# Weights loaded during layer 0's last tiles, gates kept in buffers of their own, five PSUM banks in the tail, and wider or split instructions in the rounds

## The chip, the cores and the metric

The kernel runs on one core of one Trainium2 chip. Its time is the device time of one launch in microseconds (us), taken as the median of the runs of one kernel.

A core has five engines with a program of its own each: TensorE (PE, whose weight loads are listed as PEld), VectorE (DVE), ScalarE (ACT), GpSimd (POOL) and SyncE (SP), which here only issues DMA transfers. [...]

## The reference, cut to what matters

Two layers over 16 sequences of 256 tokens with 128 features:

```python
xn = _layernorm(x)
s = _L0_attn_ref(xn, ...)               # LSTM-like scan: c = f*c + i*z, h = o*tanh(norm(c))
g = _silu(_L0_ffn_ref(xn, ...))         # tree FFN: 4 trees of depth 5, argmax over 4 children picks the row
x = x + s * g
xn = _layernorm(x)
s = _L1_attn_ref(xn, ...)               # gated delta rule, 16 heads of 8: S = S*exp(g) + k (v - kS) beta; o = qS
                                        # q, k, v = silu(conv4(xn @ W)); o * silu(xn @ Wg)
g = _silu(_L1_ffn_ref(xn, ...))         # 2 layers: local attention (8 heads of 64, window 64) and a GEGLU FFN
x = x + s * g

# inside the local attention
q = l2norm(q) * qs;  k = l2norm(k) * ksc
q = q*cos*scale + rotate_half(q)*sin*scale;  k = k*cos/scale + rotate_half(k)*sin/scale
attn = softmax(masked(8 * q @ k.T));  out = attn @ v
```

Everything is fp32.

## The kernel before, in words

**Layer 0** (`layer0_phase`, up to about 602 us, its tail to about 626). The 4096 tokens are 32 tiles of 128, in 8 groups of 4. The groups run through a software pipeline; `g` is the pipeline's step. The last two levels of the trees are not multiplied out: POOL gathers the chosen rows of a table by indirect DMA (L334, 256 of them, into `rows[4]` and `rows[5]`), DVE takes the dot products (`dots`, L753), ACT scales the rows by the activations (`gelu`, L634 and L639), and PE adds them up (`spread_rows`, L473) into `acc`. When the last group is through, its tail is a chain: ACT `tanh_f` (L676), DVE `raise_f` (L817, L818), PE `turn_f` (L480), DVE `merge` and the layer norm's statistics (`norms`, L826 to L855), ACT `put_rows` (L646, the normalised rows), PE `turn_m` (L396), ACT `keep_m` (L594), and then the projection `z` of the two gate weights on PE (L490), copied out by ACT (`keep_z`, L598) and stored by SP (L311). z(0) to z(6) belong to groups that are long done; z(7) is the last group's. They go into two PSUM banks in turn, `log_ps[h % 2]`, so that z(h) waits until keep_z(h - 2) is through. On ACT, keep_z(0) to keep_z(6) stand ahead of the last put_rows.

**Prepare** (`prepare_phase`, about 628 to 742 us). The convolution of four taps is done by PE with weights that carry the taps: DVE multiplies W and the taps into `wq`, `wk`, `wv` (L1180), and PE waits for it (`made`) before its 8 times 24 matmuls (L1025). ACT applies silu (L1052), SP stores the results to HBM scratch and loads them back in another layout (L965, L975). DVE, ACT and POOL then build the delta rule's operands, which SP stores (L982, L984). SP also issues 11 weight loads for the rounds (`m["late"]`, L994), one per step from the fourth on. At the end PE computes the output gates (L1034), ACT their silu (L1091) into buffers that alternate with the projections' staging buffers, and SP stores them (L1007). The last instruction of SP is a wait until the last gate has landed (L1015). A phase ends for all engines when all have ended (L76).

**The rounds** (`local_phase`, about 752 to 1554 us). 32 rounds, one for each of the local FFN's 2 layers and each of 16 sequences of 256 tokens, in a three-deep pipeline written out by hand: round t computes q, k, v for step t, attention for t - 1 and output projection and FFN for t - 2. POOL carries the delta rule beside it. In each round, every part is done twice (i or j = 0, 1, half of the tokens). ACT squares q and k (`squares`, L1724 and L1725); DVE rotates them (`cross` L2042 and L2043, `along` L2048, `add_parts` L2056). DVE takes the maxima of the scores (L2064), ACT the exponentials (`exps`, L1743, eight instructions over two banks), DVE the reciprocal of the sums (`inverse`, L2072) and the product (`normalise`, L2082, one instruction over both banks, after all eight). PE turns the probabilities (`turn_prob`, L1530), ACT copies them (`keep_pT`, L1751), PE multiplies by V (`weigh`, L1548), ACT copies the result (`keep_o`, L1757) out of the bank `o_ps`. That bank is then used by PE for `turn_qk` (L1482), the transposes of q, which ACT copies out (`keep_q`, L1784). `query` on DVE (L1988) is the delta rule's read-out, two instructions of 512.

## Time and profile before

| | us |
|---|---|
| median of 3 runs | 1553.08 (1552.3 to 1557.53) |
| the profiled execution | 1555.76 |
| its span, first to last instruction | 1554.0 |
| PE, DVE, ACT, POOL busy | 1306.3, 1296.0, 1235.3, 938.0 |
| layer 0 with its tail | to about 626 |
| prepare | 628.3 to 742 |
| rounds | 752 to 1554, of 23.54 each |

The page of a profile gives the busy time of each engine and, in 40 slices of the span, the busy share and the clock granted to PE. The views behind it are: windows (busy time of each engine in a stretch), the timeline (instructions in order of time, with the idle time of the engine before each and what ended it), the waits (who waited for whom), and the DMA issues (size, time to landing). L12 is line 12 of the kernel.

### The profile page before, as it was taken

The page shows a single profiled execution, that of the slowest core. Times are in us where ns is not written, and L with a number is a line of the kernel's source. Part 1 is how long each engine was busy: PE and PEld are TensorE (multiplying, and loading weights), DVE is VectorE, ACT ScalarE, POOL GpSimd, SP SyncE. Part 2 cuts the span into 40 slices and gives each one's busy share as a digit, 9 for nine tenths or more (in the row PEclk, how much of TensorE's full clock was granted, in tenths as well). Part 3 has the DMA queues.
Part 4 walks back from the last instruction along what each step waited for, and adds up shares of the span by engine and source line. Part 5 has one row for each costly group of instructions (what it writes and reads, how often), then busy time and mean ns, then how long its engine had stood idle before and what let it go on. Part 6 is the DMA issues. An engine that isn't in the chain of part 4 may idle for free.

```text
span 1554.0 us, 31376 instructions
## 1 busy us (share of the span) xinstructions
PE 1306.3 (84%) x9368; PEld 886.8 (57%) x9368; DVE 1296.0 (83%) x4362; ACT 1235.3 (79%) x3431; POOL 938.0 (60%) x1472
## 2 busy tenths in 40 slices
PE   5888878888797666897489999999999999999986
PEld 3555646566565443343256666666666666666665
DVE  3278897979888895488299999999999999999985
ACT  2367877979787886587289989989989989999985
POOL 0237464464645651078488778778778778777752
PEclk9999999999988856898699999999999999999998
DMA  3359677686868773499301101111101111111233
GB/s 111 107 183 335 222 280 248 218 297 213 314 204 285 286 274 109 136 286 315 122 22 34 44 11 44 43 44 34 43 13 44 44 44 34 19 36 44 67 94 111
DMA packets 156505, 210.33 MB, mean 135 GB/s; under 512 B 68272, under 2 KB 109616, under 8 KB 156208
## 3 DMA queue, kind: packets, MB, share of 16 engines
q0 software_dynamic: 36864, 134.76, 24.9%
q1 hardware_dynamic: 119040, 71.98, 16.8%
q8 instruction: 76, 1.25, 0.3%
q10 hardware_dynamic: 432, 1.59, 0.3%
q14 instruction: 93, 0.76, 0.2%
HBM read 168.97 MB, written 26.74 MB: 126 GB/s over the span
## 4 chain that ended last, share of the span: by engine, by line
PE 26%; ACT 14%; issue 6%; DVE 4%; POOL 2%; ACTq 0%; DVEq 0%; POOLq 0%
ACT lo_s_ps L1743 6%; PE lo_h_ps L1558 4%; PE lo_qk_ps L1454 4%; PE lo_s_ps L1510 3%; PE lo_o_ps L1548 2%; DVE prepared_then_rounds L2082 2%; ACT L1830 2%; ACT prepared_then_rounds L1801 2%; PE lo_ft_ps L1530 2%; PE lo_v_ps L1460 2%; PE lo_h_ps L1568 1%; PE lo_s_ps L1497 1%; PE lo_h_ps L1530 1%; ACT prepared_then_rounds L1751 1%; PE lo_o_ps L1530 1%
## 5 line engine op out<-in xcount | busy, mean ns | idle before, releaser
L334 POOL DMA_INDIRECT l_rows<-in_table,l_idx x256 | 256.5, 1002 | 293.9 <-DVE l_idx L795 131.4
L639 ACT ACTIVATE l_rows<-l_rows,l_act 128x128 f32<-128x128 f32 x1024 | 306.6, 390 | 2.1
L753 DVE CUSTOM_DVE_ANT_0 l_rows<-l_rows,xn_tok 128x128 f32<-128x128 f32 x1024 | 299.7, 362 | 6.5 <-DMA l_rows<-in_table,l_idx 4.9
L1743 ACT ACTIVATE lo_s_ps<-lo_s_ps,lo_nmx,lo_rn 128x128 f32<-128x128 f32 x504 | 219.7, 440 | 1.3 <-DVE lo_nmx L2066 0.9
L473 PE MATMUL l_acc<-ident,l_rows 128*128 128x128 f32 x1024 | 163.0, 307 | 55.6 <-ACT l_rows L639 34.3
L473 PEld LDWEIGHTS l_acc<-ident,l_rows 128*128 128x128 f32 x1024 | 129.4, 157 | 92.0 <-ACT l_rows L639 54.6
L439 PE MATMUL l_S<-pre,l_AT 128*128 128x144 f32 (+3 forms) x832 | 130.3, 308 | 25.9 <-ACT l_AT L630 24.7
L439 PEld LDWEIGHTS l_S<-pre,l_AT 128*128 128x128 f32 (+2 forms) x832 | 117.5, 208 | 56.4 <-ACT l_AT L630 40.0
L1454 PE MATMUL lo_qk_ps<-wqkv,lo_hT 128*128 128x512 f32 x256 | 126.6, 618 | 22.8 <-DVE lo_c L2056 11.5
L415 PE MATMUL l_log<-l_xT,top_in 128*128 128x512 f32 (+1 forms) x192 | 118.6, 711 | 19.1 <-issue 9.2
L1933 POOL TENSOR_TENSOR lo_de_kS<-lo_de_S,lo_de_ops 128x384 f32<-128x384 f32 x128 | 128.0, 1000 | 10.0
L1951 POOL TENSOR_TENSOR lo_c<-lo_c,lo_rn 128x512 f32<-128x512 f32 x64 | 66.8, 1044 | 97.1 <-ACT lo_rn L1792 94.5
L1743 ACT ACTIVATION_READ_ACCUMULATOR lo_s_ps<-lo_s_ps,lo_nmx,lo_rn 128x1 f32 x504 | 107.4, 213 | 0.0
L630 ACT ACTIVATE l_AT<-l_log,top_bias 128x512 f32<-128x512 f32 (+1 forms) x96 | 63.6, 679 | 55.0 <-PE l_log L431 48.1
L1939 POOL TENSOR_TENSOR lo_de_outer<-lo_de_dv,lo_de_ops 128x256 f32<-128x256 f32 x128 | 80.3, 628 | 10.0
L1454 PEld LDWEIGHTS lo_qk_ps<-wqkv,lo_hT 128*128 128x128 f32 x256 | 49.5, 195 | 60.4 <-issue 39.1
L2048 DVE TENSOR_TENSOR lo_qk_ps<-lo_qk_ps,tab 128x512 f32<-128x512 f32 x128 | 82.4, 690 | 0.0
L753 DVE DVE_READ_ACCUMULATOR2_ANT l_pick<- 128x1 f32 x1024 | 82.2, 80 | 0.0
L2056 DVE TENSOR_TENSOR lo_c<-lo_qk_ps,lo_c 128x512 f32<-128x512 f32 x128 | 81.7, 678 | 0.0
L2064 DVE TENSOR_REDUCE lo_nmx<-lo_s_ps 128x4 f32<-128x512 f32 x126 | 80.6, 681 | 0.0
L2021 DVE TENSOR_REDUCE lo_ss<-lo_sq 128x16 f32<-128x1024 f32 x64 | 77.3, 1207 | 3.4 <-ACT lo_sq L1725 3.4
L2082 DVE TENSOR_TENSOR prepared_then_rounds<-lo_s_ps,lo_rsum 128x1024 f32<-128x1024 f32 x63 | 77.1, 1224 | 2.3
(321 smaller groups left out, 3376.8 us busy)
## 6 DMA issues: line engine op xcount, KB each, us to landing
lo_VE<-lo_V SPq DMA_DIRECT2D x64, 128.0 KB, 2.8
scratch_ops<-prepared_then_rounds SPq DMA_DIRECT2D x4, 1792.0 KB, 7.5
lo_de_ops<-scratch_ops SPq DMA_DIRECT2D x16, 448.0 KB, 4.2
l_rows<-in_table,l_idx POOLq DMA_INDIRECT x256
scratch_qo<-prepared_then_rounds SPq DMA_DIRECT2D x8, 512.0 KB, 8.7
lo_de_qo<-scratch_qo SPq DMA_DIRECT2D x16, 256.0 KB, 4.6
x_tok<-in_x SPq DMA_DIRECT2D x8, 256.0 KB, 5.2
scratch_x<-x_tok SPq DMA_DIRECT2D x8, 256.0 KB
```

The costliest lines, as they stand in the source:

```text
L334: pool.indirect_dma_start(rows[L][:, r % SLOTS, p, :], None, a[f"table{L}"], bass.IndirectOffsetOnAxis(ap=at[:, p:p + 1], axis=0)).then_in ...
L415: ins = pe.matmul(log_ps[n % 2][0:width_of(k), :], w["top_in"][:, at_of(k):at_of(k) + width_of(k)], xT[:, h % 3, :], start=True, stop=(d = ...
L439: mm = lambda out, q, j, c0, c1, start: pe.matmul(out, at(q, j), w["top_out"][0:width_of(q), q, c0:c1], start=start, stop=True, skip_group ...
L473: ins = pe.matmul(out, rows[L][:, r % SLOTS, p, (FAN + f) * D:(FAN + f + 1) * D], m["ident"][:], start=False, stop=(L == 5 and k == PICK - ...
L639: ins = act.activation(z, z, ACT.Copy, scale=actv[L][:, r % 2, k:k + 1])
L753: ins = dve.tensor_tensor_reduce(z, z, x, 1.0, bias, ALU.mult, ALU.add, accum_out=pick[L][:, r % 2, k:k + 1])
L1454: ins = pe.matmul(dst, hT[:, u % 2, at], m["wqkv"][:, u // B, k * INNER:(k + 1) * INNER], start=True, stop=True)
L1743: ins = act.activation(here, here, ACT.Exp, scale=rn[:, v % 2, j, 2 * k + e:2 * k + e + 1], bias=nmx[:, j, e, k:k + 1], accum_out=sums[:, ...
L1933: link(pool.tensor_tensor(kS[:], both, by_key(n, U0, 3), ALU.mult))
L2048: dve.tensor_tensor(heads(src[:]), heads(src[:]), rot(u, i, a, 0, 0, DH), ALU.mult).then_inc(rotated.sem, 1)
L2056: dve.tensor_tensor(c1[:, i, w], src[:], c2[:, w], ALU.add).then_inc(done.sem, 1)
L2082: dve.tensor_tensor(prob[:, j].rearrange("p e k t -> p (e k) t"), z, rsum[:, j, :].unsqueeze(2).broadcast_to([P, 2 * NP, P]), ALU.mult).th ...
```

## The change

- At the start of ACT's program the table of the gelu functions is loaded (`preload_act_table_set`).
- In layer 0's tail z goes into five banks instead of two. z(0) to z(4) are issued by PE before the last two `spread_rows`; keep_z(0) and keep_z(1) stand between tanh_n and tanh_f, and keep_z(2) to keep_z(6) behind tanh_f as before.
- Eight of the eleven late weight loads (wqkv, wo, w1, w2, center, mean_mat, WgT, WoT: 1536 + 512 + 682 + 384 + 128 + 3 x 64 KB = 3434 KB) are issued by SP in layer 0, once spread_rows(4, 31) is done, into the memory of `rows[4]`. They stand ahead of keep_x(7). SP waits for them at the phase's end.
- The taps are multiplied into the weights by DVE in layer 0 (`weigh_taps`, three instructions), ahead of the last raise_f, in place; prepare loses these instructions, and PE the wait for them.
- In prepare, several temporaries and the gates' buffers lie in the memory of the rounds' `qT` and `kT`. ACT no longer waits for the projections' stores before a gate's silu, PE no longer waits for the late weights, and SP no longer waits for the gates' landing; that wait goes to ACT ahead of the rounds' first keep_q and to SP ahead of the load of the gates. The operands' layout in `qo` has packets of 1024 bytes where it had 512.
- In the rounds q and k are handled together: squares is one instruction of 1024 (2 of 512), cross 2 of 512 (4 of 256), along 1 of 1024 (2 of 512), add_parts 1 of 1024 (2 of 512), the maxima 1 of 1024 (2 of 512), query 1 of 1024 (2 of 512). inverse and normalise go the other way: one reciprocal of 4 and one product of 512 for each bank, each after its own four exponentials; turn_prob waits for its own bank's half.

The diff's core:

```diff
@@ layer0_phase
+        z_ps = [log_ps[0][:], log_ps[1][:], S[:, 0:2, :]..., S[:, 2:4, :]..., gate_ps[:]]
+        NZ = len(z_ps)
...
-            for h in range(3, NG):
+            for h in range(3, NG - 1):
                 keep_x(h)
+            sp.wait_ge(spread[4].sem, spread[4].after(NT - 1))
+            for k in WEIGHTS:
+                sp.dma_start(m[k], a[k]).then_inc(weights_in, 16)
+            keep_x(NG - 1)
...
+            sp.wait_ge(weights_in, 16 * len(WEIGHTS))
...
             for g in range(NG + 5):
+                for h in range(NZ) if g == NG + 3 else ():
+                    z(h)
...
-                for h in range(NG - 1) if g == NG + 4 else ():
+                for h in range(NZ, NG - 1) if g == NG + 4 else ():
                     z(h)
...
+            act.preload_act_table_set("gelu_and_others")
             act.wait_ge(halved.sem, 1)
...
                     tanh_n(g - 3)
+                for h in (0, 1) if g == NG + 2 else ():
+                    keep_z(h)
+                if on(g - 3):
                     tanh_f(g - 3)
-                for h in range(NG - 1) if g == NG + 2 else ():
+                for h in range(2, NG - 1) if g == NG + 2 else ():
                     keep_z(h)
...
+            def weigh_taps():
+                dve.wait_ge(pre_in, 16 * len([k for k in SHAPES1 if k not in PRE_EARLY]))
+                for x in "qkv":
+                    taps = m[f"conv_{x}"]
+                    dve.tensor_tensor(taps, m[f"W{x}T"].unsqueeze(1).broadcast_to([P, TAPS, P]), taps, ALU.mult)
@@ prepare_phase
-        gate_buf = [flat(stage[x][:, k]) for k in (0, 1) for x in "qkv"] + [flat(m[f"conv_{x}"]) for x in "qk"]
+        gate_buf = [m[x].rearrange("p a k t -> p (a k t)")[:, k * GW:(k + 1) * GW] for x in ("qT", "kT") for k in range(4)]
...
             sp.wait_ge(late.sem, 16 * len(m["late"]))
-            sp.wait_ge(gate_stored.sem, gate_stored.after(NG - 1))
...
-            pe.wait_ge(made.sem, 1)
...
-            pe.wait_ge(late.sem, 16 * len(m["late"]))
...
-                if g < 6:
-                    act.wait_ge(y_stored[x].sem, y_stored[x].after(n))
@@ local_phase
-                act.activation(sq[:, i, 0:INNER], q_ps, ACT.Square)
-                act.activation(sq[:, i, INNER:], k_ps, ACT.Square).then_inc(sq_ready.sem, 1)
+                act.activation(sq[:, i, :], flat(qk_ps[:]), ACT.Square).then_inc(sq_ready.sem, 1)
...
+                if (v, i) == (0, 0):
+                    act.wait_ge(m["gate_stored"].sem, m["gate_stored"].after(NG - 1))
...
-                for a, src in both:
-                    dve.wait_ge(crossed.sem, crossed.after(u, 2 * i + a + 1))
-                    dve.tensor_tensor(heads(src[:]), heads(src[:]), rot(u, i, a, 0, 0, DH), ALU.mult).then_inc(rotated.sem, 1)
+                dve.wait_ge(crossed.sem, crossed.after(u, i + 1))
+                dve.tensor_tensor(heads, heads, rot(u, i, 0, 0, DH), ALU.mult).then_inc(rotated.sem, 1)
...
+                for e in (0, 1):
+                    at, n = slice(e * NP, (e + 1) * NP), 2 * j + e + 1
...
+                    dve.wait_ge(prob_ready.sem, prob_ready.after(v, n))
+                    dve.reciprocal(rsum[:, j, at], sums[:, j, at]).then_inc(rsum_ready.sem, 1)
...
+                    dve.tensor_tensor(prob[:, j, e], z, rsum[:, j, at].unsqueeze(2).broadcast_to([P, NP, P]), ALU.mult).then_inc(pn_ready.sem, 1)
```

## Rows read from the trace of the kernel before

**Rows 1.** The page: the group of the exponentials (busy, mean ns of one).

```profile
L1743 ACT ACTIVATE lo_s_ps<-lo_s_ps,lo_nmx,lo_rn 128x128 f32<-128x128 f32 x504 | 219.7, 440 | 1.3 <-DVE lo_nmx L2066 0.9
```

**Rows 2.** Windows, one round: busy PE, PEld, DVE, ACT, POOL; PE clock, DMA share, GB/s.

```profile
1027.50:1051.04 23.54, 21.66 (x198) 15.13 (x197) 22.62 (x43) 21.35 (x62) 17.98 (x35) 1.00 0.28 70
```

**Rows 3.** Timeline, one round: start, duration, instruction, idle time before it and its releaser.

```profile
1054.39 0.20 DVE L2072 RECIPROCAL lo_rsum<-lo_sums 128x8 f32<-128x8 f32 x1 [0.39 <-ACT lo_s_ps L1743]
1054.63 0.64 ACT L1724 ACTIVATE lo_sq<-lo_qk_ps 128x512 f32<-128x512 f32 x1
1054.63 1.22 DVE L2082 TENSOR_TENSOR prepared_then_rounds<-lo_s_ps,lo_rsum 128x1024 f32<-128x1024 f32 x1
1055.60 0.64 ACT L1757 COPY prepared_then_rounds<-lo_o_ps 128x512 f32<-128x512 f32 x1
1055.79 0.42 DVE L2042 TENSOR_TENSOR lo_c<-lo_qk_ps,tab 128x256 f32<-128x256 f32 x1
1055.91 0.66 PE L1530 MATMUL lo_h_ps<-ident,prepared_then_rounds 128*128 128x128 f32 x4 [0.37 <-DVE prepared_then_rounds L2082]
1056.40 0.60 PE L1482 MATMUL lo_o_ps<-ident,lo_c 128*128 128x128 f32 x4
1057.04 0.59 ACT L1784 COPY lo_qT<-lo_o_ps 128x512 f32<-128x512 f32 x1 [0.32 <-PE lo_o_ps L1482]
1057.12 1.29 DVE L2048 TENSOR_TENSOR lo_qk_ps<-lo_qk_ps,tab 128x512 f32<-128x512 f32 x2
1062.04 2.32 DVE L1988 TENSOR_TENSOR lo_de_qS<-lo_de_S,lo_de_qo 128x512 f32<-128x512 f32 x2
```

**Rows 4.** Timeline, ScalarE at the start of the program.

```profile
9.96 1.28 ACT L646 ACT_TABLE_LOAD   x1 [9.96 <-DVE l_half L855]
```

**Rows 5.** Timeline, the end of layer 0.

```profile
607.95 0.69 DVE L817 SCALAR_TENSOR_TENSOR l_t<-l_t,l_acc 128x512 f32<-128x512 f32 x1 [7.94 <-ACT l_t L676]
610.46 8.55 PE L490 MATMUL l_log<-xT_pad,pre 128*32 128x512 f32 x14
615.85 0.16 DVE L855 SCALAR_TENSOR_TENSOR l_half<-l_mv,l_rstd 128x4 f32<-128x4 f32 x1
619.04 0.58 ACT L598 COPY xn_tok<-l_log 32x512 f32<-32x512 f32 x1 [0.34 <-PE l_log L490]
619.53 1.64 ACT L646 ACTIVATE xn_tok<-x_tok,l_half,l_rstd 128x128 f32<-128x128 f32 x4
```

**Rows 6.** Windows around the last gathers and in the steady part, columns as in rows 2.

```profile
585.00:594.00 9.00, 3.74 (x14) 2.54 (x15) 9.00 (x47) 7.20 (x23) 5.91 (x6) 0.65 0.81 291
594.00:600.00 6.00, 4.21 (x18) 3.01 (x17) 6.00 (x44) 4.30 (x15) 0.00 (x0) 0.50 0.00 1
525.00:545.00 20.00, 11.08 (x44) 7.42 (x44) 17.96 (x114) 14.05 (x44) 14.86 (x17) 0.67 0.99 368
```

**Rows 7.** Timeline, ScalarE's activations of the last two tiles' rows.

```profile
595.67 0.22 ACT L634 ACTIVATE l_act<-l_pick 128x16 f32<-128x16 f32 x1 [2.12 <-DVE l_pick L753]
601.08 0.21 ACT L634 ACTIVATE l_act<-l_pick 128x16 f32<-128x16 f32 x1
```

**Rows 8.** DMA issues: transfer, queue, count, size, us from issue to landing.

```profile
wqkv<-in_wqkv SPq DMA_DIRECT2D x1, 1536.0 KB, 7.6
```

**Rows 9.** Timeline, the start of the preparing phase.

```profile
628.34 0.69 DVE L1180 TENSOR_TENSOR pr_wq<-pre 128x512 f32<-128x512 f32 x1 [12.33 <-PEq L76]
630.29 6.26 PE L1025 MATMUL pr_ps<-xT_pad,pr_wq 128*128 128x512 f32 x8 [5.80 <-DVE pr_wv L1180]
```

**Rows 10.** SyncE's waits in 700:800: waited for, us in total, times, longest.

```profile
SPq L1015 <- DMA scratch_gate<-pre: 7.2, 1, 7.2
```

**Rows 11.** Timeline, SyncE's last issues of prepare.

```profile
740.43 2.53 SPq L1007 DMA_DIRECT2D scratch_gate<-pre  x2
```

**Rows 12.** Timeline, ScalarE: the rounds' start and their first copy of q.

```profile
751.98 1.28 ACT L1830 ACT_TABLE_LOAD   x1 [14.50 <-PEq L76]
...
769.04 0.59 ACT L1784 COPY lo_qT<-lo_ft_ps 128x512 f32<-128x512 f32 x1
```

More of the change, by code:

```diff
@@ L205, in layer0_phase @@
         idx = {4: sb("l0_idx4", [P, 2, GT * TREES], U32), 5: sb("l0_idx5", [P, SLOTS, TREES], U32)}
-        rows = {L: sb(f"l0_rows{L}", [P, SLOTS, TREES, ROW]) for L in (4, 5)}
+        rows = {4: m["wide"][:].rearrange("p (s t x) -> p s t x", s=SLOTS, t=TREES), 5: sb("l0_rows5", [P, SLOTS, TREES, ROW])}
         pick = {L: sb(f"l0_pick{L}", [P, 2, PICK]) for L in (4, 5)}
@@ L485, in z @@
                     pe.wait_ge(pre_early, 16 * len(PRE_EARLY))
-                pe.wait_ge(log_kept.sem, len(order))
+                    pe.wait_ge(log_kept.sem, len(order))
+                    pe.wait_ge(ftop_kept.sem, ftop_kept.after(NG - 1))
+                    pe.wait_ge(gate_kept.sem, gate_kept.after(NG - 1))
                 pe.wait_ge(m_kept.sem, m_kept.after(h))
-                if h >= 2:
-                    pe.wait_ge(z_kept.sem, z_kept.after(h - 2))
-                pe.matmul(log_ps[h % 2][0:2 * NH, :], m["Wab"], m["xT_pad"][:, h * SG:(h + 1) * SG, TAPS - 1:], start=True, stop=True).then_inc(z_full.sem, 1)
+                if h >= NZ:
+                    pe.wait_ge(z_kept.sem, z_kept.after(h - NZ))
+                pe.matmul(z_ps[h % NZ][0:2 * NH, :], m["Wab"], m["xT_pad"][:, h * SG:(h + 1) * SG, TAPS - 1:], start=True, stop=True).then_inc(z_full.sem, 1)
             pe.wait_ge(early, 16 * len(EARLY0))
@@ L884, in _ @@
                     dots(5, GT * (g - 3) + 0)
+                if g == NG + 3:
+                    weigh_taps()
                 if on(g - 4):
@@ L1177, in sums @@
                 dve.tensor_reduce(ss[:], sq[:], AX.X, ALU.add).then_inc(ss_ready.sem, 1)
-            for x in "qkv":
-                ins = dve.tensor_tensor(wj[x][:], m[f"W{x}T"].unsqueeze(1).broadcast_to([P, TAPS, P]), m[f"conv_{x}"], ALU.mult)
-            ins.then_inc(made.sem, 1)
             dve.wait_ge(neg_exp.sem, 1)
@@ L1415, in _ @@
             sp.wait_ge(ss_floored.sem, ss_floored.after(LAST))
+            sp.wait_ge(m["gate_stored"].sem, m["gate_stored"].after(NG - 1))
             for n in range(4):
@@ L1452, in project @@
                 at = slice(i * P, (i + 1) * P)
-                for k, dst in ((0, q_ps), (1, k_ps)):
-                    ins = pe.matmul(dst, hT[:, u % 2, at], m["wqkv"][:, u // B, k * INNER:(k + 1) * INNER], start=True, stop=True)
+                for k in (0, 1):
+                    ins = pe.matmul(qk_ps[:, k, :], hT[:, u % 2, at], m["wqkv"][:, u // B, k * INNER:(k + 1) * INNER], start=True, stop=True)
                 ins.then_inc(qk_full.sem, 1)
@@ L1465, in turn_qk @@
                 else:
-                    pe.wait_ge(q_summed.sem, q_summed.after(v, i + 1))
+                    pe.wait_ge(parts.sem, parts.after(v, i + 1))
                 dst = qk_bank(2 * i + w)
@@ L2227, in layer1 @@
         x_scope.close()
-        for k, s in SHAPES2.items():
-            if k not in ONCE2:
-                m2[k] = ctx.enter_context(nc.sbuf_tensor(k, s, F32, side="right" if k == "wqkv" else "left"))
-        m2["tab"] = ctx.enter_context(nc.sbuf_tensor("tab", [P, LAYERS, 2, 2, 2, DH], F32))
+        m2["tab"] = m["tab"].rearrange("p (l a c t j) -> p l a c t j", l=LAYERS, a=2, c=2, t=2)
         m2["b1"] = ctx.enter_context(nc.sbuf_tensor("b1_local", [P, 6 * LAYERS], F32))
@@ L2380, in program @@
             at += n
+        m["wide"] = res("wide", [P, SLOTS * TREES * ROW])
+        at = 0
+        for k, s in WIDE.items():
+            n = math.prod(s[1:])
+            m[k] = m["wide"][:, at:at + n]
+            if len(s) == 3:
+                m[k] = m[k].rearrange("p (a b) -> p a b", a=s[1])
+            elif len(s) == 4:
+                m[k] = m[k].rearrange("p (a b c) -> p a b c", a=s[1], b=s[2])
+            at += n
         gathers = keep.enter_context(Phase(nc))
+        m["gate_stored"] = Step(gathers, nc, "gate_stored", 16)
         m["x_stored"] = Step(gathers, nc, "x_stored", 16 * NG)
```

139 lines of the change are left out of this document (63 added, 76 removed).

## The prediction, made before the changed kernel ran

> **What bounds the kernel now.** The page comes first: PE and DVE are busy 84% and 83% of the span (the table above), so no engine bounds the whole, and the kernel is read by stage.
>
> The rounds are half of the span: 32 of 23.54 us. In one of them PE is busy 21.66, DVE 22.62 and ACT 21.35 us [rows 2]. None fills the period: a round is a cycle of waits across three engines, and DVE has only 0.92 us of idle time in it. The timeline shows where the waits stand [rows 3]. DVE waits 0.39 us for the last exponential, does the reciprocal and one wide normalise of 1.22, and PE waits 0.37 for that before it turns the probabilities (L1530). Next PE turns q (L1482 at 1056.40), and ACT waits 0.32 for that (L1784). But L1482 writes the bank that ACT's copy L1757 empties: the copy runs from 1055.60 for 0.64 and ends at 1056.24, 0.16 before L1482 starts.
>
> The joins are read in the timeline too. At the start ACT sits idle until 9.96 and then loads a table for 1.28 us ahead of its first rows [rows 4]. At layer 0's end the z's occupy PE for 8.55 us with 14 instructions; the norm's scaling is ready at 616.01 (615.85 + 0.16), but ACT starts put_rows only at 619.53, since the last of keep_z(0) to (6), at 619.04, stands ahead of it [rows 5]. Prepare starts at 628.34 with DVE's three products, and PE starts at 630.29 behind them [rows 9]. At its end SP waits 7.2 us for the gates' stores to land [rows 10], and nobody else works.
>
> **The change, part by part.** Minus is time saved.
>
> *Start.* The first table load moves under ACT's 9.96 us of idle time, and L646 starts 1.28 earlier [rows 4]. Layer 0 has one more load, which ran beside PE's work; it stays or goes and costs nothing either way. -1.3, bounds -1.3 and 0.
>
> *Layer 0's tail.* With five banks and z(0) to z(4) issued early, keep_z(2) to (6) run right behind tanh_f: five copies of 0.58 in the 8 us from tanh_f to 616. Put_rows starts when the scaling is ready, 616.01 and some 0.25 for the semaphore, instead of at 619.53: -3.3, with all behind it (turn_m, keep_m, z(7), its copy and store) in step [rows 5]. The two copies that now stand ahead of tanh_f take about 1.0 together, where tanh_f had waited 0.7 for PE: +0.2, bounds 0 and +0.5.
>
> The weights work against it. SP issues 3434 KB when spread_rows(4, 31) ends, at about 585, while tile 31's gathers are under way: from 585 to 594 the DMA engines move 291 GB/s, 2.6 MB, and then nothing, so the gathers land by about 593.5 [rows 6]. Their first readers are tile 31's dot products, which follow tile 30's; ACT takes up tile 30 at 595.67 and tile 31 at 601.08, the second without idle time before it [rows 7]. A tile's dots take some 4.4 us, so they may start at 596.7 and delay nobody: that is when the gathers are needed. If both streams get half of the engines until the gathers are through, these land after 5.2 MB. At the 368 GB/s of the steady part [rows 6] that is 14 us from 585, 599, a loss of 2.4; at 291 it is 603, a loss of 6; if the weights queue up behind, nothing. The weights have longer rows than the gathers' mix, so I lean to the quick side and take +2.0, bounds 0 and +6. They are all down by 610 at worst (a landing of 1536 KB took 7.6 us [rows 8]), well ahead of the phase's end. keep_x(7), which SP now issues behind eight more transfers, isn't due before 612.
>
> [...]
>
> weigh_taps is three instructions, the 1.95 us between 628.34 and 630.29 in prepare [rows 9]. In layer 0 DVE runs them between the last dots, at 600, and raise_f, before which it sits idle 7.94 us [rows 5]: 0, and 1.95 if that cover were gone. The whole tail: -3.3 + 0.2 + 2.0 = -1.1, bounds -3.3 and +3.
>
> *Prepare's start.* PE starts right with the phase instead of 1.95 later [rows 9], and follows on without a gap until its projections are through: -1.95. The last fifth of prepare belongs to DVE and POOL, fed through loads; with 3.4 MB less in the queues it may close up a bit more, or soak up a part. Bounds -1 and -3.
>
> *The gates' landing.* The phase ends with SP's last issue, 740.43 + 2.53 = 742.96 [rows 11], and the wait of 7.2 us goes [rows 10]. Next late are DVE and PE, which are through at 741.5. The wait comes back on ACT ahead of the rounds' first keep_q, but that copy starts 17 us after the rounds do, 769.04 against 751.98 [rows 12], and the gates land 7.2 us after SP's last issue: covered by 8 us. Behind it on ACT stand all copies of the first rounds, so without the cover it would cost the full wait. -7.2, bounds -8 and -6.5.
>
> *The rounds.* Four exponentials of 0.44 with their read-outs take 1.8 us [rows 1]: the first bank's are done 1.8 before the second's. DVE's earlier work ends at 1054.00 (0.39 before 1054.39), so the first half of normalise (0.20 and some 0.65) is ready at about 1054.95 instead of 1055.85, and PE's wait of 0.37 is gone [rows 3]. The second half is ready as before, over 2 us ahead of its reader. PE then comes to L1482 at about 1056.03, but the bank is free at 1056.24, or 0.05 earlier, as two squares of 0.64 (1054.63 to 1055.60, 0.97) become one of 1024, which I put at 0.92. So L1482 moves from 1056.40 to about 1056.24, and ACT's next copy with it: -0.16.
>
> Against that stands DVE's sum. A pair of 512 takes 1.29, one product of 1024 takes 1.22 [rows 3]: the split costs 0.07 and a second reciprocal of 0.20, twice a round, +0.55. The merging gives back 0.07 each for along, add_parts and the maxima (twice) and for query, and about 0.1 for cross, whose four of 256 take 1.33 (1055.79 to 1057.12), twice: -0.7. Net about -0.1, beside 0.92 of idle time. along now waits for both halves of cross: 0 to +0.1. 30 rounds of 0.16 are -4.8; bounds 0 and -9 (0.30 a round).
>
> *Ramp, last rounds, clock.* Normalise by bank helps where PE waits for it in the first and last rounds, 0.4 each, and PE's shorter pause between the phases may save 0.3 of slow clock: -1.1, bounds 0 and -2.
>
> Sum: -1.3 - 1.1 - 1.95 - 7.2 - 4.8 - 1.1 = -17.4. Against the profiled execution, 1555.76, that is 1538.3; it lay 2.7 above the median of the runs, and 1.8 of it lie outside its span. Against the median, 1553.08, it gives 1535.7, and I say **1536**.
>
> **The rivals.**
>
> 1. *The weights take the gathers' time.* Tile 31's rows land at 603, and the tail is +3 instead of -1.1: 1536 + 4.2 = 1540. For it: the gathers get no more than 291 GB/s when alone [rows 6]. Against: 368 at other times, and the order of issue, since most of the gathers are on their way before the weights. [...]
>
> 2. *The rounds gain PE's whole wait.* 30 times 0.37 = 11.1 in place of 4.8: 1529.5. It needs L1757 to move up with the rest. Against: ACT's instructions from 1054.63 on follow each other without idle time up to 1056.7 [rows 3], so only shorter work can move it.
>
> 3. *The rounds gain nothing.* The split uses up DVE's 0.92, or the merged instructions wait for the later of q and k: 1536 + 4.8 = 1541.
>
> 4. *Slower: DVE becomes the bound.* The wide instructions may take more than the sum of their parts. Query is the place to look: two of 512 took 2.32 together, beside POOL [rows 3], and it becomes one over broadcast operands. Outside the rounds 12.6 us are gained. The rounds must get longer by 0.4 us each, 12.6 / 32, to bring the time back to 1553, and by 0.54 to be slower by 0.3%. With 0.92 of idle time to fill first, DVE's work must grow by 1.3 to 1.5 us a round; about 16 us of it are touched, so by 8 or 9%. Then the time is 1558 and more.
>
> 5. *The join gives less.* SP's last issues took 1.27 each (2.53 for two [rows 11]); if the queues push back as hard without the weights' late loads, or more since the gates now come sooner, the end moves by 4 instead of 7.2: 1539.
>
> **How the numbers follow.** The forecast, 1533 to 1538.5: 0.48. Rival 1: 0.14. Rival 2: 0.10. Rival 3: 0.13. Rival 5: 0.07. Rival 4: 0.05. A smaller growth of DVE's work that eats most of the gain: 0.03. The range reaches toward rival 2's side and beyond rivals 1 and 3, to where one of them meets a weak join: 1528 to 1544. A measurement of this kernel can tell 0.3%, 4.7 us, from no change. Faster than 1548.4 are the forecast and rivals 1, 2, 3 and 5, 0.92, less 0.02 for two of them together: 0.90. Within: 0.05. Slower: 0.05.
>
> **What would show it.** In the profile of the changed kernel: no load between 9.96 and ACT's first rows; put_rows 0.25 behind the scaling; tile 31's dots with or without a wait for a DMA, the tail's whole question; PE's first L1025 right at the phase's start; no wait of SP for the gates, and 2 us from its last issue to the rounds; a period of 23.38 with L1530 not waiting for normalise and L1482 right behind the end of L1757. The prediction is wrong if the period is over 23.5 or under 23.2, if DVE has no idle time left in a round, or if ACT waits over 3 us for tile 31.

## The result, and where the time went

The changed kernel takes 1542.23 us (median of 4 runs, 1538.92 to 1543.03) where the kernel before takes 1553.03, 10.8 us less. The ratio on record is 0.9917, 95% interval 0.9888 to 0.9945; the two medians by themselves give 0.9930, inside it. On another chip, where the kernel before took 1521.53, the changed kernel took 1508.75, 12.8 less, and the ratio was 0.9924 (0.9901 to 0.9946). The gain is clear of the noise, and under 1%. The forecast was 1536, range 1528 to 1544. The direction and the range held; the gain is 0.6 of the forecast one.

The page of the changed kernel, busy time by engine:

```profile
span 1541.0 us, 31140 instructions
PE 1294.8 (84%) x9368; PEld 881.3 (57%) x9368; DVE 1270.8 (82%) x4138; ACT 1228.2 (80%) x3366; POOL 945.8 (61%) x1472
```

The time is read by stage, from marks in the timelines: the last two `tanh_f` of layer 0, the start of prepare, the end of SyncE's last issue in prepare, the rounds' first instruction, and the table load that opens each round. The first column needs a word: it is 571 and 581 us in two profiles of the kernel before, and 565 and 533 in two of the changed kernel, so layer 0's body wanders by more than this change is worth. The later stages agree far better. "28 rounds" is from the fourth round's table load to the last one's, "period" the mean of the ten rounds from the eleventh on, "end" from the last round's table load to the end of the span.

| profile | last but one tanh_f | to the last | to prepare | prepare | join | first 3 rounds | 28 rounds | period | end |
|---|---|---|---|---|---|---|---|---|---|
| before | 571.3 | 36.0 | 21.0 | 114.7 | 9.0 | 62.0 | 659.6 | 23.544 | 80.5 |
| before_again | 580.6 | 36.1 | 20.7 | 114.1 | 9.6 | 63.9 | 659.5 | 23.542 | 80.6 |
| before_preload | 576.4 | 36.1 | 21.2 | 114.8 | 9.1 | 61.9 | 659.3 | 23.533 | 80.6 |
| changed | 564.7 | 42.9 | 18.1 | 112.5 | 2.0 | 62.1 | 657.5 | 23.484 | 81.3 |
| changed_again | 533.5 | 42.9 | 18.1 | 112.6 | 2.0 | 61.8 | 657.1 | 23.467 | 79.5 |
| no_preload | 570.9 | 43.2 | 18.0 | 113.3 | 1.8 | 62.0 | 657.1 | 23.467 | 80.3 |
| split_only | 537.3 | 36.1 | 19.2 | 114.7 | 8.6 | 62.1 | 660.1 | 23.593 | 80.3 |
| merged_only | 576.8 | 41.3 | 18.1 | 113.3 | 1.8 | 62.4 | 659.7 | 23.569 | 80.4 |
| one_normalise | 587.1 | 42.6 | 18.1 | 112.8 | 1.8 | 62.6 | 661.6 | 23.629 | 81.1 |
| weights_after_gathers | 578.6 | 36.3 | 18.1 | 112.6 | 2.0 | 62.0 | 657.2 | 23.469 | 79.1 |
| weights_in_prepare | 576.1 | 36.3 | 18.1 | 111.9 | 2.0 | 61.9 | 654.0 | 23.357 | 81.2 |
| keep_o_first | 578.4 | 42.5 | 18.1 | 111.9 | 2.0 | 62.0 | 654.0 | 23.358 | 79.2 |
| both_moves | 534.8 | 36.7 | 18.1 | 113.0 | 1.8 | 61.9 | 654.0 | 23.355 | 80.0 |
| keep_k_first | 535.7 | 36.2 | 18.1 | 112.5 | 1.9 | 63.9 | 658.4 | 23.503 | 80.2 |

From the mean of the first three rows to that of the next three: +6.9 in the interval to the last tanh_f, -2.9 to prepare, -1.7 in prepare, -7.3 at the join, -2.2 in 28 rounds, and in the first rounds and the end nothing beyond their own scatter of 1 to 2. With -1.4 at the program's start that is -8.6. The medians say -10.8 and -12.8; the rest, 2 to 4 us, is not in these stages. It would lie in layer 0's body, where it is not told apart from the wander, and no run shows its cause.

Single rounds can mislead here. A few are longer than their neighbours by 0.33 to 0.36 us: one each in before, before_again and before_preload, one in split_only, two in merged_only, none in the changed kernel. So 0.3 of the 2.2 above is one long round. The long round of split_only and one of merged_only's fall into the ten of the period; without them the two periods are 23.559 and 23.533. What makes a round long was not looked into. Two rounds of merged_only as windows (columns as in rows 2), an ordinary and a long one:

```profile
978.76:1002.30 23.54, 21.65 (x202) 15.15 (x200) 21.35 (x33) 21.21 (x59) 18.39 (x35) 1.00 0.30 71
1072.90:1096.79 23.89, 21.65 (x202) 15.15 (x200) 21.83 (x33) 21.21 (x59) 18.15 (x35) 1.00 0.31 70
```

**The start.** ScalarE starts its first rows at 9.82; before, a table load stood there at 9.96 [rows 4]:

```profile
9.82 1.65 ACT L658 ACTIVATE xn_tok<-x_tok,l_half,l_rstd 128x128 f32<-128x128 f32 x4 [6.37 <-DVE l_half L876]
```

**Layer 0's end.** The timeline of the changed kernel, and the windows of the same stretch. SyncE issues the first weights at 578.38, behind spread_rows(4, 31) and 0.67 after POOL's first gather of tile 31. VectorE then stands 7.63 us for tile 31's gathers, ScalarE 6.58 behind it; in before ScalarE took that tile up with no idle time [rows 7].

```profile
577.71 0.94 POOL L341 DMA_INDIRECT l_rows<-in_table,l_idx  x1 [2.69 <-DVE l_idx L817]
...
578.38 0.35 SPq L311 DMA_DIRECT2D wide<-in_wqkv  x1
583.60 0.54 SPq L311 DMA_DIRECT2D wide<-in_WoT  x1
...
596.66 0.35 DVE L768 CUSTOM_DVE_ANT_0 l_rows<-l_rows,xn_tok 128x128 f32<-128x128 f32 x1 [7.63 <-DMA l_rows<-in_table,l_idx]
...
601.03 1.89 DVE L839 TENSOR_TENSOR pre<-pre 128x512 f32<-128x512 f32 x3
...
601.14 0.21 ACT L646 ACTIVATE l_act<-l_pick 128x16 f32<-128x16 f32 x1 [6.58 <-DVE l_pick L768]
607.54 0.58 ACT L688 ACTIVATE l_t<-l_acc 128x512 f32<-128x512 f32 x1
...
616.07 0.16 DVE L876 SCALAR_TENSOR_TENSOR l_half<-l_mv,l_rstd 128x4 f32<-128x4 f32 x1
...
616.26 1.65 ACT L658 ACTIVATE xn_tok<-x_tok,l_half,l_rstd 128x128 f32<-128x128 f32 x4 [2.04 <-DVE l_half L876]
```

```profile
588.00:591.00 3.00, 0.44 (x4) 0.37 (x4) 1.02 (x8) 1.91 (x7) 0.00 (x0) 1.00 1.03 422
591.00:594.00 3.00, 2.00 (x11) 1.19 (x9) 0.00 (x0) 3.00 (x12) 0.00 (x0) 0.72 1.01 400
594.00:597.00 3.00, 1.21 (x5) 0.72 (x4) 0.34 (x3) 0.56 (x2) 0.00 (x0) 0.50 0.39 130
```

What the DMA queues carried (packets, MB, share of 16 engines): q1 has the weights, q0 the gathers. First from 577 to 598, with the landing of the largest weight, then in two parts of it, 580 to 586 and 588 to 592:

```profile
q1 hardware_dynamic: 1152, 3.52, 45.0%
q0 software_dynamic: 875, 3.16, 39.7%
wide<-in_wqkv SPq DMA_DIRECT2D x1, 1536.0 KB, 10.1
...
q1 hardware_dynamic: 122, 1.42, 66.3%
q0 software_dynamic: 136, 0.51, 25.5%
...
q1 hardware_dynamic: 209, 0.89, 53.8%
q0 software_dynamic: 215, 0.78, 48.3%
```

In both parts the two queues move nearly as many packets as each other. From 580 to 586 the weights' packets are of 11.6 KB on the average and the gathers' of 3.8 KB, so the gathers get only 0.51 of 1.93 MB; from 588 to 592 both are near 4 KB and the bytes are shared about evenly. The DMA engines are at 400 GB/s and more from 588 to 594, where before they moved 291 on the average and then nothing [rows 6]. VectorE's first dot product of tile 31 starts at 596.66, 18.3 us after the first weight was issued; before, the gathers by themselves had landed within 8.5 to 9 us of the same point (585 to about 593.5 [rows 6]). The rest of the tail went nearly as forecast: the taps' products run at 601.03 in idle time, and put_rows starts 0.03 after the scaling's last instruction ends (616.07 + 0.16), where it had waited 3.5 [rows 5].

What the whole tail gains depends on the clock granted to PE. split_only has the tail of the kernel before, and its stretch to prepare takes 19.2 instead of 20.7 to 21.2: z(0) to z(6) take 7.64 at a mean clock of 0.82, where before has 8.55 at 0.73. The last group's projection z(7) in before, split_only and the changed kernel:

```profile
622.60 1.88 PE L490 MATMUL l_log<-xT_pad,pre 128*32 128x512 f32 x2 [0.72 <-issue]
587.79 1.02 PE L490 MATMUL l_log<-xT_pad,pre 128*32 128x512 f32 x2 [0.72 <-issue]
619.75 1.92 PE L499 MATMUL l_S<-xT_pad,pre 128*32 128x512 f32 x2 [0.68 <-ACT xT_pad L606]
```

The granted clock was 0.50 in the first and third stretch and 1.00 in the second. In every profile with the new tail z(7) took 1.91 or 1.92; with the other z's issued early PE stands idle for 4.36 us ahead of turn_m in the changed kernel, where it had been 2.22. The clock went from 1.00 to 0.50 within that idle time (at 616.2, PE's work having ended at 613.6), and in before at 621.8, as turn_m ended; what lowered it no run shows. Against the one old tail whose last projection ran at 1.00 the gain is 1.1 us and not 2.9.

**The join.** PE starts with the phase, 625.64 against 625.61, and the rounds begin 2.0 after SyncE's last issue (735.49 + 2.60), where it had been 9.0 [rows 9 to 12]:

```profile
625.64 2.04 PE L1045 MATMUL pr_ps<-xT_pad,pre 128*128 128x512 f32 x2 [3.98 <-PEq L76]
...
735.49 2.60 SPq L1029 DMA_DIRECT2D scratch_gate<-wide  x2
...
740.09 1.28 ACT L1845 ACT_TABLE_LOAD   x1 [7.77 <-PEq L76]
```

**The rounds.** One round of the changed kernel as a window (columns as in rows 2), then its timeline, which answers to rows 3:

```profile
1037.02:1060.50 23.48, 21.62 (x202) 15.15 (x199) 21.78 (x37) 21.23 (x59) 18.25 (x35) 1.00 0.01 1
```

```profile
1041.57 0.17 DVE L2084 RECIPROCAL lo_rsum<-lo_sums 128x4 f32<-128x4 f32 x1
1041.77 0.69 DVE L2089 TENSOR_TENSOR prepared_then_rounds<-lo_s_ps,lo_rsum 128x512 f32<-128x512 f32 x1
...
1042.28 1.07 ACT L1738 ACTIVATE lo_sq<-lo_qk_ps 128x1024 f32<-128x1024 f32 x1
1043.19 0.62 ACT L1770 COPY prepared_then_rounds<-lo_o_ps 128x512 f32<-128x512 f32 x1
1043.66 0.65 ACT L1791 COPY wide<-lo_ft_ps 128x512 f32<-128x512 f32 x1
1044.63 0.59 ACT L1799 COPY wide<-lo_o_ps 128x512 f32<-128x512 f32 x1 [0.32 <-PE lo_o_ps L1496]
...
1043.03 0.60 PE L1544 MATMUL lo_h_ps<-ident,prepared_then_rounds 128*128 128x128 f32 x4
1043.96 0.63 PE L1496 MATMUL lo_o_ps<-ident,lo_c 128*128 128x128 f32 x4 [0.34 <-ACT prepared_then_rounds L1770]
...
1049.46 1.21 DVE L2002 TENSOR_TENSOR lo_de_qS<-lo_de_S,lo_de_qo 128x1024 f32<-128x1024 f32 x1
...
1049.62 1.91 POOL L1948 TENSOR_TENSOR lo_de_kS<-lo_de_S,lo_de_ops 128x384 f32<-128x384 f32 x1
```

PE's wait for normalise (0.37 ahead of L1530 [rows 3]) is gone: the same instruction, now L1544, follows without one. But the next instruction of PE, the turn of q (L1496), now waits 0.34 for ScalarE's copy L1770, which ends at 1043.81. Counted from the round's table load this turn starts at 6.94 us, where it had started at 7.03. That is all that the round gained. VectorE works 0.84 less a round (21.78 against 22.62 [rows 2]), and the period falls by only 0.06.

### The profile page after: what moved, and what is told of

Read it like the earlier page. It is cut to its first block, busy times and chain, and to the rows that moved or that the text cites. A ratio compares the mean times of both kernels' runs of the same rounds, so it can differ in the third digit from the quotient of the medians.

```text
span 1541.0 us, 31140 instructions
## 1 busy us (share of the span) xinstructions
PE 1294.8 (84%) x9368; PEld 881.3 (57%) x9368; DVE 1270.8 (82%) x4138; ACT 1228.2 (80%) x3366; POOL 945.8 (61%) x1472
## 4 chain that ended last, share of the span: by engine, by line
PE 26%; ACT 17%; issue 6%; DVE 2%; POOL 1%; ACTq 0%; DVEq 0%; POOLq 0%
ACT lo_s_ps L1756 5%; PE lo_qk_ps L1468 4%; PE lo_h_ps L1572 4%; PE lo_s_ps L1524 3%; PE lo_o_ps L1562 3%; ACT L1845 2%; ACT prepared_then_rounds L1816 2%; PE lo_ft_ps L1544 2%; ACT prepared_then_rounds L1770 2%; ACT lo_sq L1738 2%; PE lo_v_ps L1474 2%; PE lo_h_ps L1582 1%; PE lo_s_ps L1511 1%; ACT prepared_then_rounds L1764 1%; PE lo_o_ps L1496 1%
## 5 line engine op out<-in xcount | busy, mean ns | idle before, releaser
L341 POOL DMA_INDIRECT wide<-in_table,l_idx x128 | 129.6, 1012 | 204.2 <-DVE l_idx L810 128.7
L341 POOL DMA_INDIRECT l_rows<-in_table,l_idx x128 | 126.8, 990 | 81.9 <-DVE l_idx L817 45.7
L768 DVE CUSTOM_DVE_ANT_0 wide<-wide,xn_tok 128x128 f32<-128x128 f32 x512 | 155.9, 368 | 6.5 <-DMA wide<-in_table,l_idx 5.0
L651 ACT ACTIVATE l_rows<-l_rows,l_act 128x128 f32<-128x128 f32 x512 | 153.1, 387 | 1.0
L651 ACT ACTIVATE wide<-wide,l_act 128x128 f32<-128x128 f32 x512 | 153.1, 387 | 1.0
L768 DVE CUSTOM_DVE_ANT_0 l_rows<-l_rows,xn_tok 128x128 f32<-128x128 f32 x512 | 145.1, 347 | 7.6 <-DMA l_rows<-in_table,l_idx 7.6
L1468 PE MATMUL lo_qk_ps<-wide,lo_hT 128*128 128x512 f32 x256 | 127.4, 621 | 18.6 <-DVE lo_c L2065 12.3
L422 PE MATMUL l_log<-l_xT,top_in 128*128 128x512 f32 (+1 forms) x192 | 118.8, 712 | 16.7 <-ACT l_AT L642 10.8
L480 PE MATMUL l_acc<-ident,l_rows 128*128 128x128 f32 x512 | 80.3, 301 | 31.9 <-ACT l_rows L651 29.0
L2089 DVE TENSOR_TENSOR prepared_then_rounds<-lo_s_ps,lo_rsum 128x512 f32<-128x512 f32 x126 | 87.1, 691 | 4.3
L1045 PE MATMUL pr_ps<-xT_pad,pre 128*128 128x512 f32 x192 | 84.7, 603 | 4.0 <-PEq L76 4.0
```

The source lines that it names most:

```text
L341: pool.indirect_dma_start(rows[L][:, r % SLOTS, p, :], None, a[f"table{L}"], bass.IndirectOffsetOnAxis(ap=at[:, p:p + 1], axis=0)).then_in ...
L422: ins = pe.matmul(log_ps[n % 2][0:width_of(k), :], w["top_in"][:, at_of(k):at_of(k) + width_of(k)], xT[:, h % 3, :], start=True, stop=(d = ...
L480: ins = pe.matmul(out, rows[L][:, r % SLOTS, p, (FAN + f) * D:(FAN + f + 1) * D], m["ident"][:], start=False, stop=(L == 5 and k == PICK - ...
L651: ins = act.activation(z, z, ACT.Copy, scale=actv[L][:, r % 2, k:k + 1])
L768: ins = dve.tensor_tensor_reduce(z, z, x, 1.0, bias, ALU.mult, ALU.add, accum_out=pick[L][:, r % 2, k:k + 1])
L1045: ins = pe.matmul(bank[k][:], wj[x][:, j, :], m["xT_pad"][:, 8 * g:8 * g + 8, c * CT + j:(c + 1) * CT + j], start=(j == 0), stop=(j == TAP ...
```

## The experiments

Theories: **W**, the weights' transfers hold up tile 31's gathers and cost the tail some 6 to 7 us. **O**, the round is held by the bank `o_ps`, which ScalarE's keep_o empties, and not by normalise. Rivals: late gathers of their own, a round held by VectorE, and layer 0's wander or the table load as the source of what the stages don't explain. The experiments ran in three groups, each beside the kernel before on a chip of its own, where that kernel took 1566.9, 1521.5 and 1557.8; times are against it. before_again, split_only and merged_only were run once each, for their profiles; their times prove nothing.

**before_again**, no edit.

> The kernel before, unchanged, for a second profile. In the profile of the changed kernel layer 0 was already 1.4 us ahead at the first tile's copy (14.17 against 12.73), as forecast for the table load, but 4.3 to 4.9 us ahead from the sixth group on and 6.6 at spread_rows(4, 31), for which nothing in the change accounts. Theory A, the gathers' stage wanders from one execution to the next: this profile will put the eight l_xT copies at times other than 14.17, 44.31, 89.11, 145.83, 214.09, 281.58, 349.02, 415.30, by 2 us or more in the later ones. Theory B, the change made layer 0 itself faster: they come within 0.5 us of those times.

1566.93 us. The eight l_xT copies of layer 0 came at 13.93, 42.42, 87.82, 149.35, 218.60, 286.47, 356.08 and 423.66, up to 8.4 later than in the first profile, while the rounds' period was 23.542 against 23.544. So theory A: layer 0's body wanders by itself, between chips and between executions (on this chip the kernel before took 1562.18 to 1571.41); a difference there between two profiles says nothing about the change.

**weights_after_gathers.**

```diff
             sp.wait_ge(spread[4].sem, spread[4].after(NT - 1))
+            last = got[5][(NT - 1) % SLOTS]
+            sp.wait_ge(last.sem, last.after((NT - 1) // SLOTS))
             for k in WEIGHTS:
```

> The changed kernel, with one more wait on SyncE ahead of the eight weight transfers: for the landing of tile 31's gathers. Theory A, the weights took the gathers' share of the DMA engines: VectorE's wait of 7.6 us for a DMA ahead of tile 31's dot products goes, the gathers land within 7 us of their issue, the weights still land before the phase ends (3.4 MB in about 9 us, from about 587), and the time falls by 6 to 8 us, to about 1535. Theory B, the gathers of tile 31 were late for another reason (their own issue, or the long row of 526 KB each): the wait stays at 5 us or more and the time moves by less than 2. Theory C, the weights now end last: the phase's end waits for them and the gain is half or less.

Ratio 0.9904 (0.9872 to 0.9937), 15.1 less. Its timeline: the weights go out at 601.86, when the last gather is in, and ScalarE takes up tile 31 without idle time.

```profile
601.86 0.34 SPq L313 DMA_DIRECT2D wide<-in_wqkv  x1
...
608.47 0.22 ACT L648 ACTIVATE l_act<-l_pick 128x16 f32<-128x16 f32 x1
```

The interval to the last tanh_f is 36.3, against 36.1 before the change and 42.9 in the changed kernel: W holds, worth 6.6. The weights are down before the phase ends (tanh_f to prepare is 18.1 as in the changed kernel), so the third theory falls. The medians of this group are too noisy (the five of this variant spread over 11 us) to show 6.6 between variants; the stage shows it.

**keep_o_first.**

```diff
-                if on(t):
-                    squares(t, 0)
                 if on(t - 2):
                     keep_o(t - 2, 0)
+                if on(t):
+                    squares(t, 0)
```

> The changed kernel with ScalarE's keep_o(t - 2, 0) ahead of squares(t, 0) in the rounds, nothing else. In the changed kernel PE no longer waits for normalise but waits 0.34 us for keep_o before it turns q into the same bank, and the period went from 23.54 to 23.48 only. Theory A, the bank that keep_o empties is what holds the round: the turn of q starts 0.45 earlier, ScalarE's wait for it goes or shrinks, the period falls to 23.0 to 23.1 and the time by 12 to 15 us, to about 1528 to 1530. VectorE's cross then starts 0.45 later, which its 1.7 us of idle time takes. Theory B, the round is held by VectorE or by ScalarE's sum: the wait moves to another place and the period stays within 0.1 of 23.48, the time within 3 us.

Ratio 0.9916 (0.9886 to 0.9945), and a period of 23.358: 0.125 less than the changed kernel's, not the 0.4 expected. The timeline of a round:

```profile
1053.66 0.63 ACT L1770 COPY prepared_then_rounds<-lo_o_ps 128x512 f32<-128x512 f32 x1
1054.14 1.08 ACT L1738 ACTIVATE lo_sq<-lo_qk_ps 128x1024 f32<-128x1024 f32 x1
1055.05 0.64 ACT L1791 COPY wide<-lo_ft_ps 128x512 f32<-128x512 f32 x1
...
1054.85 0.60 PE L1496 MATMUL lo_o_ps<-ident,lo_c 128*128 128x128 f32 x4
1055.79 0.41 PE L1511 MATMUL lo_s_ps<-mask,ident 64*64 64x512 bf16 x4 [0.34 <-issue]
...
1055.25 0.69 DVE L2054 TENSOR_TENSOR lo_c<-lo_qk_ps,wide 128x512 f32<-128x512 f32 x1 [0.59 <-ACT lo_sq L1738]
```

The turn of q waits for nothing and starts 6.44 after the table load (1048.41), 0.50 earlier. But the scores, L1511, start only 0.12 earlier and have 0.34 in front of them; the copy of k (L1791), now behind squares, ends at 1055.69, 0.10 before. So O holds for this wait, but it was worth 0.12 a round and no more: something else then holds the round, by this row the copy of k.

**one_normalise.**

```diff
-                for e in (0, 1):
-                    ... reciprocal of 4, product of 512 for bank e, each then_inc(..., 1)
+                dve.wait_ge(prob_ready.sem, prob_ready.after(v, n))
+                dve.reciprocal(rsum[:, j, :], sums[:, j, :]).then_inc(rsum_ready.sem, 2)
+                ...
+                dve.tensor_tensor(prob[:, j]..., z, rsum[:, j, :]..., ALU.mult).then_inc(pn_ready.sem, 2)
```

> The changed kernel with normalise again one reciprocal of 8 and one product of 1024 after all eight exponentials; the merged instructions for q and k stay. Theory A, the split took PE's wait of 0.37 away but only 0.06 of it counted, since keep_o stood right behind: the period is 23.5 to 23.55 and the time 2 us above the changed kernel's, about 1544. Theory B, the split was worth its full 0.37 and something else in the change cost 0.3 a round: the period is 23.8 and the time 10 us above.

Ratio 0.9961 (0.9942 to 0.998), period 23.629: between the two theories. PE waits 0.45 for normalise. One part of it was the variant's own: the product started 0.10 after the reciprocal's end (1066.31 + 0.20).

```profile
1066.31 0.20 DVE L2083 RECIPROCAL lo_rsum<-lo_sums 128x8 f32<-128x8 f32 x1 [0.42 <-ACT lo_s_ps L1756]
1066.61 1.22 DVE L2088 TENSOR_TENSOR prepared_then_rounds<-lo_s_ps,lo_rsum 128x1024 f32<-128x1024 f32 x1
```

**merged_only**: the same with `then_inc(..., 1)` and the waits counted as in before.

> The changed kernel with normalise in one again, now with increments of one as in the kernel before. In one_normalise the two wide normalise instructions incremented their semaphores by two, and the product started 0.10 after the reciprocal's end where before it had been 0.04, so its period of 23.63 may hold 0.08 of the variant's own. Theory A, the two gates of the round stand side by side (normalise at 7.03 us after the round's start in before, keep_o's copy at 7.01 with the split alone and 6.94 with the merged squares): the merging alone frees only VectorE and the period is 23.54, as before. Theory B, the merging alone costs: 23.6 or more.

1555.65 us, period 23.569, and 23.533 without the long round that lies in its ten, where before has 23.544. The product starts 0.03 after the reciprocal's end (983.79 + 0.20, 984.02), and PE waits 0.37 for it as before. So theory A holds: the merging alone saves 1.2 us of VectorE's time a round and, within 0.01, no time of the round's. The 0.10 a round between one_normalise and this variant is then the increments' and their waits'.

**split_only**: the kernel before with normalise by bank alone.

> The kernel before with normalise by bank alone; squares, cross, along, add_parts, the maxima and query stay in halves, and everything outside the rounds stays. Theory A, the split takes PE's wait of 0.37 but PE then waits for keep_o's copy, and only 0.05 to 0.07 a round are won, and the merging is worth nothing: the period is 23.47 to 23.50. Theory B, the split was worth more and the merging cost it again: the period is 23.3 or less. Theory C, the split is worth nothing and the merging made the 0.06: the period is 23.54.

Period 23.593, and 23.559 without its long round: theory A fails, and of the three C comes nearest. A round as a window, and the turn of q in its timeline:

```profile
990.15:1013.74 23.59, 21.69 (x202) 15.19 (x200) 22.96 (x48) 21.40 (x61) 18.04 (x35) 1.00 0.30 72
```

```profile
996.16 0.60 PE L1530 MATMUL lo_h_ps<-ident,prepared_then_rounds 128*128 128x128 f32 x4
997.16 0.63 PE L1482 MATMUL lo_o_ps<-ident,lo_c 128*128 128x128 f32 x4 [0.40 <-ACT prepared_then_rounds L1757]
...
996.58 0.42 DVE L2042 TENSOR_TENSOR lo_c<-lo_qk_ps,tab 128x256 f32<-128x256 f32 x1 [0.18 <-ACT lo_sq L1725]
```

PE no longer waits for normalise, waits 0.40 for keep_o instead, and turns q 7.01 after the round's table load where before it was 7.03. VectorE is now at 22.96 of 23.59 and its cross starts later. So the two gates stood side by side: with the split alone nothing is won (it ends 0.015 above before), with the merging alone 0.01. Together they give 0.06 to 0.08. The merged squares let keep_o's copy end, and the turn of q start, 0.07 earlier (6.94). That VectorE's freed time pays for the split is likely by these sums, but no run shows it by itself.

**changed_again**, no edit, beside the next two.

> The changed kernel, unchanged, on the chip and beside the kernel before of this job. Layer 0 wanders by up to 9 us between profiles of one kernel, but the rounds' period did not (23.54 and 23.54 in two profiles of before), so stages are compared by their own lengths: period 23.48, the stretch from the last group's tanh_f in layer 0 with a wait of VectorE for a DMA of about 7 us ahead of tile 31's dot products, prepare 112.5 us, 2.0 from SyncE's last issue to the rounds. Time 9 to 13 us under before.

1508.75 us, ratio 0.9924 (0.9901 to 0.9946). Every stage is as in the first profile within 0.4, but for the end (1.8 less) and layer 0's body (31 less).

**both_moves**: both edits that helped.

> The changed kernel with both single edits that helped: SyncE waits for tile 31's gathers before it issues the weights, and keep_o(t - 2, 0) stands ahead of squares(t, 0). If they are independent (one is in layer 0, the other in the rounds), the gains add: 6 us of the tail and 30 times 0.125 = 3.8 in the rounds, so about 10 under the changed kernel and about 20 under before; period 23.34 to 23.36. If the waits elsewhere take it back, it stays within 6 of the changed kernel.

1500.64 us, ratio 0.9866 (0.9837 to 0.9895): 20.9 under before and 8.1 under changed_again. The stages give 9.3 of them: 6.2 in the tail, 3.1 in 28 rounds. This version beats both kernels.

**keep_k_first**: both_moves with keep_k(t - 1, 0) ahead of squares(t, 0) too.

> both_moves with ScalarE's keep_k(t - 1, 0) ahead of squares(t, 0) as well. In keep_o_first the turn of q started 0.50 earlier but the scores only 0.12 earlier: they waited 0.34 us, and the copy of k ended 0.10 before they started, pushed back by squares. Theory A, the copy of k is what holds the scores: they start about 0.3 earlier and the period falls by 0.1 to 0.3, to 23.05 to 23.25. Theory B, squares and the second copy of q, now 0.6 later, hold something else back (VectorE's cross, the second probabilities): the period stays or grows.

1508.48 us, period 23.503, all of keep_o_first's gain gone: theory B. VectorE's cross waits for the squares:

```profile
987.77 0.69 DVE L2057 TENSOR_TENSOR lo_c<-lo_qk_ps,wide 128x512 f32<-128x512 f32 x1 [1.81 <-ACT lo_sq L1740]
```

The scores did start earlier (6.97 after the round's table load, 7.38 in keep_o_first), but the 1.81 of VectorE went into the maxima and from there into the next exponentials, which now wait 0.2 for them in each round. ScalarE's queue at this place has three consumers, PE twice and VectorE, and squares may not fall further back.

**before_preload**: the kernel before with the early table load alone; **no_preload**: the changed kernel without it.

> The kernel before with the early load of the gelu table alone. What is open: from the stages' own lengths (last group of layer 0 to the end) the changed kernel is 6.4 us faster in the first pair of profiles, and the medians say 10.8 and 12.8; 1.4 of the rest is the table at the start, and some 3 to 5 stay without a cause in layer 0's body. Theory A, the early load is worth 1.3 to 1.4 and no more, and the rest is wander of the gathers' stage or belongs to another part: this kernel is 1 to 2 us under before. Theory B, the early load shifts layer 0 and is worth the rest too: 4 to 6 under before.

> The changed kernel without the early load. Theory A (the load is worth 1.3 to 1.4): 10 to 12 us under before, the first l_xT copy at 14.1. Theory B (it also moves layer 0's body): 6 to 8 us under before.

0.9989 (0.9969 to 1.0009), 2.3 less, and 0.9938 (0.9908 to 0.9968), 9.4 less. The first l_xT copy stands at 12.85 with the load moved and at 14.12 without: 1.3, and no sign in the stages that it is worth more. Theory A fits better, but the two intervals reach to 4.8 and down to 5.0 us less, so the times don't exclude B. The 2 to 4 us between the stages' sum and the medians keep no cause shown.

**weights_in_prepare**: both_moves (so with keep_o first) with the eight weights in prepare's list again.

> both_moves with the eight weights loaded in prepare again, one per step as in the kernel before, and PE waiting for them ahead of the gates. Theory A, the layer 0 tail doesn't need them and prepare is bound by PE, so that only the place matters in that it must not meet tile 31's gathers: the tail is 36.0 to 36.7 between the last two tanh_f, prepare 112.5 to 113.5, and the time is within 2 us of 20 under before. Theory B, 3.4 MB in prepare fill the DMA queues and prepare gets longer by 1.5 or more (before it was 114.1 to 114.7, of which 1.95 are the products at its start).

1536.78 us, ratio 0.9878 (0.9847 to 0.991), 21.1 under before. Prepare is 111.9, no longer than with the weights gone, so theory A holds. no_preload, in the same group, took 1548.4; the 11.6 between them are the stages' 6.9 in the tail, 3.1 in 28 rounds and 1.3 at the start, so here the medians show the tail's loss too. Moving the weights into layer 0 was worth nothing in prepare and cost 6.6 in the tail: of the changes outside the rounds this one is a loss.

## Why the prediction was right, and where it was not

The forecast was 1536, its core 1533 to 1538.5; 1542.23 is outside that core and 1.8 inside the end of the range. Part of this is luck: the stages' own -8.6 would have given 1544.4, just outside, and the rest came from layer 0's body, of which the prediction says nothing. By its own signs it was wrong in one point, "if ACT waits over 3 us for tile 31": ScalarE waited 6.58. And the period, 23.48, is nearer to the 23.5 that would have refuted it than to 23.38.

*Start*, -1.3: the copies show 1.3 to 1.4. *z in five banks*, -3.3 + 0.2: measured -2.9 in the column "to prepare" and +0.2 in the one before it (36.3 against 36.1, with the weights out of the way), and only -1.1 against the old tail whose last projection ran at a clock of 1.00, which the prediction did not reckon with. Put_rows follows the scaling by 0.03 and not by the 0.25 that the prediction allows for the semaphore, which no row of before shows (in its whole trace the same hand-over takes 0.04 at 36.05, 200.08 and 466.24, and 0.31 at 267.21); the cover for the taps' products was there. *Conv weights*, -1.95: -1.7. The hope that prepare would close up with fewer DMAs was not met. *The gates' landing*, -7.2: -7.3, and nobody waits for it later; rival 5 is out. The cover was worked out too small: from the prediction's own numbers it is 17 + 2 - 7.2, near 12 us and not 8. The first keep_q starts at 757.35, and the last gate, issued near 737, lands 8.8 later.

*The weights*, +2.0: they cost 6.6. The mechanism was right, the place too (tile 31's dots, 1 us of slack: a wait of 7.6 became a loss of 6.6), the size was wrong. The step that failed is "the weights have longer rows than the gathers' mix, so I lean to the quick side". The rows were longer, but that is a reason for the slow side: while the longest were under way, 580 to 586, the gathers got 0.51 MB of 1.93. From the first weight's issue to 596.66, when tile 31's dots could start, the queues carried 3.51 MB of weights instead of the 2.6 of "half of the engines", beside 2.59 MB of gathers: 6.1 MB at 334 GB/s are 18.3 us. The 18 that I had worked out for the slow bound came from 5.2 MB at 291, two errors that cancel. This part of rival 1, given 0.14, is what happened. How two large streams share the engines stood in no row of before; in this trace the two queues moved nearly as many packets as each other, 122 against 136 and 209 against 215.

*The rounds*, -4.8: -2.2, of which 0.3 is the absence of a long round. The step that failed is "the bank is free at 1056.24". I took the end of keep_o's copy as the moment from which PE could start, and the 0.16 up to L1482 as slack. It was the time that PE took to start after a copy it waits for: in the changed kernel PE waits for that same copy and starts 0.15 after its end (1043.81, 1043.96), in split_only 0.14 after (997.02, 997.16). So keep_o nearly bound L1482 in the kernel before already, with a slack of 0.02 (split_only, with normalise out of the way, turns q 0.02 earlier), and only the merged squares could move it further. By that 0.02 + 0.07 a round would have been forecast, 30 x 0.09 = 2.7.

*Ramp, last rounds, clock*, -1.1: nothing that stands out of a scatter of 1 to 2. The 0.3 of slow clock in it was the author's estimate and no row shows it. PE's first stretch of work in the rounds ran at a granted clock of 0.50 before and 0.51 after the change, and took 5.49 (from 752.48) and 5.47 us (from 740.58).

With these three terms set right the sum is -17.4 + 4.6 + 2.6 + 1.1 = -9.1, near the stages' -8.6. VectorE's sum was wrong too, in the harmless direction: forecast about -0.1 a round, measured -0.84, since query went from 2.32 to 1.21, while POOL's product beside it went from 1.00 to 1.91. Rival 4 was far off.

## What to carry to other kernels

Where PE waited for ScalarE's copy it started 0.14 to 0.15 us after the copy's end (split_only, changed kernel), and in before, with another releaser listed, 0.16 after it. A consumer that starts so close behind a producer may well be bound by it; look for the second gate right behind the first before pricing its removal. Transfers that are brought forward into a stage's last loads can hold these up: here they took 0.89 of 1.67 MB where both had packets of about 4 KB, and 1.42 of 1.93 where theirs were of 11.6 KB against 3.8, and cost 6.6 us. So hold them until the loads have landed, or leave them where they are hidden already. Where one stage wanders by more than the change is worth, compare the stages' own lengths, and look at the single rounds before trusting a mean of ten.
